# Message phase of a graph network: the second norm's offset is added to the target rows by TensorE in PSUM, and VectorE's one-hot of edge types stands last in its turn

## The reference, cut to what matters

```python
def _L1_gnn_ref(x, edge_index, edge_type, edge_emb_W, msg_W, msg_b, upd_W, upd_b, ln_g, ln_b):
    src, dst = edge_index
    et = edge_emb_W[edge_type]                        # 16 types, 32 wide
    m = relu(concat([x[src], et], -1) @ msg_W.T + msg_b)
    agg = segment_sum(m, dst, num_segments=50000) / clip(deg, 1.0)[:, None]
    h = x + (agg @ upd_W.T + upd_b)
    mu, var = mean(h), var(h)                         # over the 128 features
    return (h - mu) * rsqrt(var + 1e-5) * ln_g + ln_b

x = _layernorm(x + _L1_gnn_ref(x, ...))               # second norm of the phase
```

## Time and profile before

| what | value |
|---|---|
| median of 3 runs | 2641.88 us (2640.07 to 2645.51) |
| the profiled execution | 2639.84 us |
| its span, first to last instruction | 2638.0 us |
| mean granted TensorE clock | 0.764 |
| PE, DVE, ACT, POOL busy, share of the span | 54%, 61%, 33%, 71% |
| first gather of the message phase | 700.06 us |
| last statistic rows of the phase turned (L1428) | 1114.08 us |
| first gather of the next phase | 1145.88 us |

### The profile page before, as it was taken

The page is one execution under the profiler, slowest core; times in us unless marked ns, Lnnn a source line. Parts: engine busy times, 40 slices in busy tenths (PEclk is TensorE's granted clock), DMA queues, the critical chain, the costliest instruction groups (busy, mean ns, idle before and its releaser), DMA issues. The chain is left out here.

```text
span 2638.0 us, 21630 instructions
## 1 busy us (share of the span) xinstructions
PE 1425.5 (54%) x4580; PEld 731.6 (28%) x4580; DVE 1606.3 (61%) x4851; ACT 863.9 (33%) x1813; POOL 1861.6 (71%) x1494
## 2 busy tenths in 40 slices
PE   6787588887266666546777456444554650011211
PEld 1443244444122222212333234222222330011110
DVE  8899387788258878938777544333334554434443
ACT  0111266677235566634665511111111320000000
POOL 5773878775388886254677687777874868878787
PEclk9899799999577777768898778777777875555555
DMA  1111344443435454343454467577696873333331
GB/s 25 28 33 40 95 118 121 125 112 81 96 75 126 124 129 128 93 102 88 109 127 115 89 169 194 158 168 192 180 157 184 226 202 94 86 67 70 74 72 43
DMA packets 350927, 297.90 MB, mean 113 GB/s; under 512 B 103741, under 2 KB 305228, under 8 KB 350781
## 3 DMA queue, kind: packets, MB, share of 16 engines
q1 hardware_dynamic: 253197, 225.40, 31.1%
q0 software_dynamic: 97600, 71.11, 14.3%
HBM read 199.75 MB, written 96.70 MB: 112 GB/s over the span
## 5 line engine op out<-in xcount | busy, mean ns | idle before, releaser
L2081 PE MATMUL tl_pX<-k_ident,tl_ga 125*128 125x125 f32 x400 | 84.2, 348 | 445.7 <-DMA tl_ga<-table_TE,k_s_idxE 332.0
L2192 DVE TENSOR_TENSOR_SCAN tl_S<-tl_same,tl_S,tl_pX 128x500 f32<-128x500 bf16 x96 | 120.3, 1254 | 315.9 <-PE tl_pX L2081 178.7
L471 POOL DMA_INDIRECT tl_ga<-table_TE,k_s_idxE x200 | 244.7, 1224 | 63.4 <-issue 59.4
L2081 PEld LDWEIGHTS tl_pX<-k_ident,tl_ga 125*128 125x128 f32 x400 | 57.3, 177 | 461.9 <-DMA tl_ga<-table_TE,k_s_idxE 342.1
L471 POOL DMA_INDIRECT eq_ga<-table_T,k_idxS x100 | 124.8, 1248 | 81.9 <-ACT eq_y L1786 52.9
L471 POOL DMA_INDIRECT ms_ga<-table_T,k_idxS x100 | 132.9, 1329 | 51.6 <-issue 42.0
L471 POOL DMA_INDIRECT tl_ga<-table_TH,k_send x100 | 122.7, 1227 | 58.7 <-issue 57.8
L1261 PE MATMUL tl_pCon<-dr_BC,dn_cT 128*128 128x512 f32 x196 | 135.0, 778 | 52.9 <-ACT dn_cT L1268 29.2
L471 POOL DMA_INDIRECT at_ga<-x,k_src x100 | 131.8, 1318 | 43.4 <-issue 25.2
L273 POOL DMA_INDIRECT table_ptab<-k_ef,ix_scatI x100 | 125.1, 1251 | 45.6 <-issue 45.6
L2032 POOL DMA_INDIRECT result<-tl_o,k_dst_end x100 | 121.8, 1218 | 44.3 <-issue 29.3
(11 more groups left out here) (464 smaller groups left out, 4455.0 us busy)
## 6 DMA issues: line engine op xcount, KB each, us to landing
dr_x<-x SPq DMA_DIRECT2D x97, 256.0 KB, 7.7
result<-dr_o SPq DMA_DIRECT2D x97, 256.0 KB, 5.1
dm_xT<-xT SPq DMA_DIRECT2D x32, 768.0 KB, 6.2
table_T<-at_y SPq DMA_DIRECT2D x50, 250.0 KB
table_T<-ms_y SPq DMA_DIRECT2D x50, 250.0 KB
table_T<-eq_y SPq DMA_DIRECT2D x50, 250.0 KB
table_TE<-tl_y SPq DMA_DIRECT2D x50, 250.0 KB
tl_fac<-table_dinv SPq DMA_DIRECT2D x50, 250.0 KB, 4.7
```

What stands on the lines that cost most here:

```text
L471: nc.gpsimd.indirect_dma_start(out=buf[:, k, :], out_offset=None, in_=table, in_offset=bass.IndirectOffsetOnAxis(ap=index[:, CT * c + k:CT ...
L2081: last = nc.tensor.transpose(pX[j % 2][:, k * TP:(k + 1) * TP], ga[j % RG][:, k, :], K["ident"][0:TP, 0:TP])
L2192: nc.vector.tensor_tensor_scan(S[i][:], same[j % RM][:], pX[i][:, 0:CE], 0.0 if j % NC == 0 else S[1 - i][:, CE - 1:CE], ALU.mult, ALU.add ...
```

## The change

`xb` keeps the source rows only (its buffers are halved), and GpSimd adds the offset to these alone. For the target rows a new step `biased(c)` on TensorE multiplies the identity with the loaded rows (512 columns) and then a row of ones with the offset row repeated four times (`lbrow`, 512 columns) into one of two new PSUM banks `pB`. It stands between `update` and the moments, and waits for the loaded rows and, as the bank is read by the add two chunks before, for `h2(c-2)`. VectorE's add of 125x1024 (L1562) becomes two of 125x512, the first reading PSUM. SP makes four more loads of 512 bytes ahead of the broadcast rows, and all engines wait for 11 loads instead of 7. `one_hot(s+3)` moves from behind `running(s)` to the end of VectorE's turn.

```diff
-        xu, xb = ([a.sb(f"{n}{i}", [TP, 2 * CT, D]) for i in range(RU)] for n in ("xu", "xb"))
+        xu, xb = ([a.sb(f"{n}{i}", [TP, k * CT, D]) for i in range(RU)] for n, k in (("xu", 2), ("xb", 1)))
+        lbrow, onerow = a.sb("lbrow", [1, CT * D]), a.sb("onerow", [1, TP])
...
+        pB = [a.ps(f"pB{i}", [128, 512]) for i in range(2)]
+        s_xbT, s_one = a.sem("xb_targets"), a.sem("one_row")
...
+            for k in range(CT):
+                sp.dma_start(lbrow[:, k * D:(k + 1) * D], g["rowv"][3:4, :]).then_inc(s_w, 16)
             for t, r in ((ub, 1), (lg, 2), (lb, 3)):
...
             def load_targets(c):
-                need(sp, s_xb, c - RX + 1)
+                need(sp, s_xbT, c - RX + 1)
                 need(sp, s_h1, c - RX + 1)
...
-            pool.wait_ge(s_w, 16 * 7)
+            pool.wait_ge(s_w, 16 * 11)
...
             def biased(c):
                 i = c % RU
                 have(pool, c)
-                pool.wait_ge(s_xt[c % RX], 16 * (c // RX + 1))
                 need(pool, s_h2, c - RU + 1)
-                nc.gpsimd.tensor_tensor(xb[i][:, 0:CT, :], xt[c % RX][:], bc(lb, CT), ALU.add)
-                nc.gpsimd.tensor_tensor(xb[i][:, CT:2 * CT, :], ga[c % RG][:], bc(lb, CT), ALU.add).then_inc(s_xb, 1)
+                nc.gpsimd.tensor_tensor(xb[i][:], ga[c % RG][:], bc(lb, CT), ALU.add).then_inc(s_xb, 1)
...
+            def biased(c):
+                i = c % 2
+                pe.wait_ge(s_xt[c % RX], 16 * (c // RX + 1))
+                need(pe, s_h2, c - 1)
+                nc.tensor.matmul(pB[i][0:TP, :], K["ident"][0:TP, 0:TP], xt[c % RX][:].rearrange("p k f -> p (k f)"), start=True, stop=False)
+                nc.tensor.matmul(pB[i][0:TP, :], onerow[:], lbrow[:], start=False, stop=True).then_inc(s_xbT, 1)
...
                 if live(s):
                     update(s)
+                    biased(s)
                     dn.moments(pe, MA + s)
...
         def _(dve):
+            nc.vector.memset(onerow[:], 1.0).then_inc(s_one, 1)
...
                 need(dve, s_y, c - 1)
-                nc.vector.tensor_tensor(h2[c % 2][:], hg[:], xb[c % RU][:], ALU.add).then_inc(s_h2, 1)
+                dve.wait_ge(s_xbT, c + 1)
+                nc.vector.tensor_tensor(h2[c % 2][:, 0:CT, :], hg[:, 0:CT, :], pB[c % 2][0:TP, :].rearrange("p (k f) -> p k f", k=CT), ALU.add)
+                nc.vector.tensor_tensor(h2[c % 2][:, CT:2 * CT, :], hg[:, CT:2 * CT, :], xb[c % RU][:], ALU.add).then_inc(s_h2, 1)
...
                 if live(s):
                     running(s)
-                if live(s + 3):
-                    one_hot(s + 3)
...
                 if live(s - 1):
                     scale(s - 1, mv1, sd1, rs1, nb1, s_sd1, s_rs1, s_r1, s_n1)
+                if live(s + 3):
+                    one_hot(s + 3)
```

More of the change, by code:

```diff
@@ L1400, in _ @@
         def _(pe):
-            pe.wait_ge(s_w, 16 * 7)
+            pe.wait_ge(s_w, 16 * 11)
             nc.tensor.matmul(pM[0:16, 0:D], emb[:], We[:], start=True, stop=True).then_inc(s_tw, 1)
             pe.wait_ge(s_twc, 1)
+            pe.wait_ge(s_one, 1)
             def turn(c):
@@ L1447, in _ @@
             act.wait_ge(s_eps, 1)
-            act.wait_ge(s_w, 16 * 7)
+            act.wait_ge(s_w, 16 * 11)
             def source(c):
@@ L1509, in _ @@
             dve.wait_ge(s_eps, 1)
-            dve.wait_ge(s_w, 16 * 7)
+            dve.wait_ge(s_w, 16 * 11)
             def one_hot(c):
```

## The result

The changed kernel takes **2689.01 us** (median of 4 runs, 2686.32 to 2690.10) against 2640.98 for the kernel before on the same chip (4 runs, 2636.76 to 2645.51): ratio **1.018** [1.0161, 1.0199], 48 us slower. The forecast was 2649, slower by 7.7, and its range ended at 2665. The sign and the closing loop were right, the size was a sixth of the true one.

A forecast was written before the change was run, and what follows sets the result against it. The loop of DVE, ACT and PE bounds, POOL close behind. Turn 4 opening 1.5 earlier, then -0.6, -1.05, +9.85 and +1.0 make +7.7: profiled 2639.84 to 2647.5, median 2.0 above, so 2649 us; range 2613 to 2665.

The forecast's parts named there:

- the closing loop: PE's wait for DVE's `h2` closes the loop `one_hot`'s move opens: `h2` at r (PE's turn opening) + 7.55, idle 3.7 us.
- rival 1: TensorE's clock doesn't fall, or only briefly, while PE waits for `h2`: -34 us, 2608; half the dip 2630; chance 0.20.
- `biased` and the moments, 6.9 + 2.7 = 9.6: PE's 16 instructions behind the wait for `h2`: 6.9 us at the high clock plus 2.7 for the low clock.
- turns A, B and C: PE's turns with s % 4 of 0, 1 and 2: forecast 18.25 us for the first, 17.15 for each other.
- My bounds, 6.9 and 10.3: Range in us for PE's `biased` plus moments: all at the high clock, or a low clock for eight instructions.
- D: PE's turn with s % 4 of 3, four short transposes instead of moments: forecast 11.9 us, against 15.0 before.
- The start: SP's four more issues ahead of the rows delay the message phase's start by 1.45 us.
- The first turns: Before turn 4: two or three POOL adds and one stall on `mean` less, -3 us; turn 4 opens 1.5 earlier.
- Rival 2: POOL was the bound after all in the message phase and PE's wait hides: -18 us, 2624; chance 0.10.
- The loop bounds, and POOL is close behind: Kernel before, message phase: the DVE, ACT and PE loop sets the pace, 64.6 us per four turns, POOL not ahead.
- Rival 3: POOL's remaining add stalls DVE's `gained` and add of `h2`: up to 1.5 us a turn, 2666; chance 0.15.
- `one_hot` out of POOL's way: DVE's `one_hot`, up to 3676 ns when meeting POOL's two adds: half the POOL add halves long stalls, earning nothing extra.

The follow-up runs named there:

- the cured ones: Changed kernel with a third `pB` buffer (0.9866), with `biased` behind the moments (0.9857), or with both (0.9875), ratios to the kernel before.

## Why the prediction was right in kind and wrong in size

- **The loop that closes again: right.** `h2` at r + 7.64 (forecast 7.55), PE's idle of 4.1 us in most turns (3.7), `one_hot` without its wait in the steady turns, POOL idle before its gathers (87.5 us). Removing the wait alone (three buffers) turns +48 us into -35 us.
- **The low clock behind PE's idle (rival 1): right to fear it.** In the 23 turns from turn 2 on, PE idles 2.48 to 5.75 us before `biased`. In 16 of them the first pair takes 2.04 us, the level of 1.2 GHz; in the other 7 it takes 1.38 to 1.90, so the clock falls within it; and the second pair is at the low level in all 23. Rival 1 is refuted.
- **The term that failed: `biased` and the moments, 6.9 + 2.7 = 9.6.** It measured 12.2, 10.6 and 11.9 in turns A, B and C. The 2.7 for the low clock came from the 12 moments of the earlier trace rows, products over 128 rows, and I took it to hold for any 16 instructions behind an idle. With one product over one row among them the low stretch lasts about 7 to 9.2 us instead of 5.2. A smaller part is the spacing of the pairs: at the high clock throughout the term is 7.24 (752.10 to 759.34) instead of 6.9, and at the low level the second pair takes 2.0 (950.20 to 952.20) instead of 1.71. With 125 rows the term measures 9.6. My bounds, 6.9 and 10.3, were both drawn from full products, so the upper end was no bound for this one.
- **D: right.** 11.9 forecast, 12.4 and 12.3 measured. D ends at the low clock and the next turn, A, starts in it; I had allowed 0.5 for that, and `h2` comes at r + 8.95 (939.28 to 948.23) against my 8.65. A is 21.2 us, not 18.25, but nearly all of that is again the term above (12.2 instead of 9.6).
- **The start: right, +1.3** (first gather's idle 7.74 against 6.42; forecast 1.45). The first turns: wrong. Of the +6.9 at turn 4, 2.9 lie ahead of the phase; +4.0 stand against my -1.5. The 27.1 us of turn 2 hold a wait of 6.79 for a gather (below), then `h2`, then a low stretch to 783.5; I had counted the adds saved on POOL but not that the closed loop is paid there too.

```profile
766.74 1.10 PE L1413 MATMUL ms_pA<-k_ident,ms_ga 125*128 125x125 f32 x4 [6.79 <-DMA ms_ga<-table_T,k_idxS]
```

- **Rival 2 (POOL bounds): refuted for this kernel**, shown for the cured ones, whose group of 58.9 to 59.3 us is four times POOL's 14.75.
- **"The loop bounds, and POOL is close behind": not borne out for the kernel before.** I read the 51.3 us of DVE's wait as what moving `one_hot` could give. With the move alone, turns 4 to 16 gained 0.8 us, as POOL's turn was as long as the loop's. It cost the sum nothing, since PE's wait closed the loop again.
- **Rival 3 (stalls of `gained` and the add of `h2`): refuted.** `gained` took at most 1.23 us in all 25 chunks and the half add from PSUM at most 0.69, as the prediction had it for an add with one operand in PSUM; the half add with both operands in SBUF took 0.68 at the median and 2.18 at most. `gained` and the first half add in a steady turn:

```profile
931.78 1.23 DVE L1569 TENSOR_TENSOR ms_hg<-ms_n,ms_lg 125x1024 f32<-125x1024 f32 x1 [1.09 <-ACT ms_n L1486]
933.04 0.69 DVE L1576 TENSOR_TENSOR ms_h<-ms_hg,ms_pB 125x512 f32<-125x512 f32 x1
```

- **`one_hot` out of POOL's way: right**: its longest is 512 ns, was 3676. Being last was worth 0.5% by itself, as said.

```profile
L1528 DVE TENSOR_SCALAR ms_oneh<-ms_typ,ms_kindf x25: 460/467/512, 704.4 to 1115.0; 16x500 f32<-16x500 int32 x25
```

The 2637 to 2660 that the forecast gave itself would have held the kernel with 125 rows (2659.16, on a chip whose kernel before took 2645.72); it did not hold the change as written.

## What to carry to other kernels

A step with a wait goes behind the independent work of its turn, or gets one more buffer: here either edit takes the ratio from 1.018 to under 0.987, where the change as written had made it slower. A long wait of one engine is no gain to be had while another has no idle left: 51.3 us of waiting gave 0.8 us in twelve turns. When an engine is made to wait inside its turn, cost what is queued behind the wait, and at the clock at which TensorE restarts. A cheap-looking product over one row is not a cheap filler behind an idle: take its price from a row of the trace with as few occupied rows, and where there is none, put the upper bound well above that of full products.

## What the hardware did that I had not expected

Behind the same idle of 4.1 us, the same number of instructions over the same columns came back to the high clock after 5.25 us with a second product over 125 rows, and after about 7 to 9.2 us with one over 1 row; zeros in 124 of 125 rows didn't change it. The Trainium skill, TensorE: Matmul & The Clock Gate, section What's actually happening, says that the clock follows how busy the array has lately been, and that no count of instructions decides. The second agrees with this case, the counts being equal here (1.018 against 1.0048). On the first, the profile shows PE without idle in both stretches, so its busy time alone doesn't tell them apart. Why 32 rows behave almost as one and 64 only a little better stays open; the spacing of the pairs has the same step between 64 and 125 rows.

The length of an idle alone didn't decide either whether it ended low: 2.48 and 2.74 us did in the changed kernel (pairs of 2.04 us at 774.25 and 948.23), while 3.31 and 3.33 us ended high with 64 rows (1.09 us at 806.64 and 946.64).
